# A mixture of experts over all experts, replaced by sorted pairs of token and expert with gathered rows

## The reference, cut to what matters

```python
def _L0_ffn_ref(x, Wr, br, W1, b1, W2, b2, ln_g, ln_b):     # D_MODEL = 768, D_HID = 192, N_EXP = 8
    logits = jnp.einsum('bsd,de->bse', x, Wr) + br
    probs = jax.nn.softmax(logits, axis=-1)
    top_vals, top_idx = jax.lax.top_k(probs, TOP_K)          # TOP_K = 2
    routing_weights = top_vals / jnp.sum(top_vals, axis=-1, keepdims=True)
    onehot = jax.nn.one_hot(top_idx, N_EXP, dtype=x.dtype)
    expert_weights = jnp.einsum('bsk,bske->bse', routing_weights, onehot)
    h = jax.nn.gelu(jnp.einsum('bsd,edh->besh', x, W1) + b1[None, :, None, :])
    y = jnp.einsum('besh,eho->beso', h, W2) + b2[None, :, None, :]
    out = jnp.einsum('beso,bse->bso', y, expert_weights)
    mu = jnp.mean(out, axis=-1, keepdims=True)
    var = jnp.mean(jnp.square(out - mu), axis=-1, keepdims=True)
    return (out - mu) * jax.lax.rsqrt(var + LN_EPS) * ln_g + ln_b
...
x = x + _L0_ffn_ref(_layernorm(x, axis=-1)[None], ...)[0]
```

## Time and profile before

| | us |
|---|---|
| median of 3 runs | 4639.31 (4627.12 to 4641.16) |
| profiled execution, its own time | 4635.16 |
| profiled execution, span from first to last instruction | 4633.4 |
| TensorE busy in the span | 3928.1 (85%) |
| VectorE busy | 2149.3 (46%) |
| GpSimd busy | 1350.2 (29%) |
| ScalarE busy | 1170.5 (25%) |
| mean granted clock of TensorE | 0.913 of 2.4 GHz |
| moved by DMA | 729.54 MB |

### The profile page before, as it was taken

One profiled execution on the slowest core, in us unless ns is written; L12 is line 12 of the kernel. 1 busy time (PEld: TensorE's weight loads), 2 busy tenths in 40 slices (PEclk: granted clock), 3 DMA queues, 4 the chain that ended last, 5 costly groups with the idle time before them and its releaser, 6 DMA issues. The chain is left out here.

```text
span 4633.4 us, 67390 instructions
## 1 busy us (share of the span) xinstructions
PE 3928.1 (85%) x23483; PEld 3147.0 (68%) x23484; DVE 2149.3 (46%) x4835; ACT 1170.5 (25%) x2391; POOL 1350.2 (29%) x1368
## 2 busy tenths in 40 slices
PE   6764988898989499996999578888878849999998
PEld 6763666666666288886999544554545449999997
DVE  6852555555555444443222144444444444444544
ACT  1231333333333233332111022222222122222222
POOL 1113655555556100000000144554555301111110
PEclk8886999999999799998999778888888969999999
DMA  5764666666676333334566466777777430000000
GB/s 207 255 247 140 222 208 216 212 216 216 215 223 215 118 139 135 140 124 127 80 80 77 151 226 220 257 250 238 259 229 241 148 117 21 27 20 20 27 20 13
DMA packets 239565, 729.54 MB, mean 157 GB/s; under 512 B 75503, under 2 KB 80650, under 8 KB 230995
## 3 DMA queue, kind: packets, MB, share of 16 engines
q0 software_dynamic: 88000, 374.95, 25.4%
q1 hardware_dynamic: 151315, 351.47, 25.0%
HBM read 642.07 MB, written 145.41 MB: 170 GB/s over the span
## 5 line engine op out<-in xcount | busy, mean ns | idle before, releaser
L873 POOL DMA_INDIRECT k_rows<-tab,k_pick x576 | 593.1, 1030 | 455.8 <-PE k_num L1293 307.7
L1996 POOL DMA_INDIRECT m_rows<-tab,m_e x500 | 486.6, 973 | 502.1 <-PE m_out L2295 313.7
L1293 PE MATMUL k_num<-k_rows,k_wt 128*64 128x385 f32 (+1 forms) x2400 | 435.8, 509 | 43.5 <-issue 38.6
L1293 PEld LDWEIGHTS k_num<-k_rows,k_wt 128*64 128x64 f32 x2400 | 171.8, 141 | 257.5 <-issue 239.7
L2275 PE MATMUL m_pj<-m_w,m_at 128*128 128x384 f32 x600 | 253.6, 582 | 28.8 <-DVE m_x L2091 22.7
L133 PE MATMUL g_prod<-g_w_hi,g_h_h 128*128 128x384 f32 x800 | 269.5, 337 | 1.5 <-DVE g_h_l L1594 1.5
L135 PE MATMUL g_prod<-g_w_hi,g_h_l 128*128 128x384 f32 x800 | 267.5, 334 | 0.0
L134 PE MATMUL g_prod<-g_w_lo,g_h_h 128*128 128x384 f32 x800 | 267.3, 334 | 0.0
L2295 PE MATMUL m_out<-m_rows,m_wt 128*32 128x384 f32 x2000 | 239.7, 513 | 22.7 <-issue 22.0
L133 PE MATMUL f_prod<-f_w_hi,f_a_h 128*128 128x512 f32 x600 | 243.9, 406 | 0.0
L2071 DVE TENSOR_REDUCE m_mx<-m_dash 128x2 f32<-128x512 f32 x150 | 103.0, 687 | 285.8 <-remote 205.5
(11 more groups left out here) (292 smaller groups left out, 8927.1 us busy)
## 6 DMA issues: line engine op xcount, KB each, us to landing
agg<-k_outb SPq DMA_DIRECT2D x100, 384.0 KB
f_a_in<-agg SPq DMA_DIRECT2D x100, 384.0 KB
h<-f_e SPq DMA_DIRECT2D x25, 1024.0 KB, 4.1
g_h<-h SPq DMA_DIRECT2D x25, 1024.0 KB, 12.9
tab<-q_xn SPq DMA_DIRECT2D x25, 388.5 KB, 6.0
tab<-g_row SPq DMA_DIRECT2D x25, 385.5 KB, 4.7
m_own<-tab SPq DMA_DIRECT2D x25, 385.5 KB
q_x<-in_x SPq DMA_DIRECT2D x25, 384.0 KB, 5.9
```

Of the source, the lines that this page charges most:

```text
L873: pool.indirect_dma_start(rows[:, place(u, n), :], None, dram["tab1"], at, bounds_check=bound, oob_is_err=False).then_inc(rows_in[i], 16)
L1293: mm = pe.matmul(num[i][64 * g:64 * g + 64, 0:n], wt[:, 2 * c + g, :], rows[:, place(u, 2 * c + g), a:a + n], start=(c == 0), stop=(c == 2 ...
L1996: pool.indirect_dma_start(rows[:, place(h, c) + k, :], None, tab, bass.IndirectOffsetOnAxis(ap=e[h % 4][:, 0, k * SLOTS + c:k * SLOTS + c ...
```

## The change

`phase_i` goes, and `phase_ffn` takes its place with three phases, each with a `Pool` and so a barrier of its own. All their loops are written out, with no loop instruction.

`phase_route` (tiles `r_`): for each of the 25 token tiles, layer norm, six transposes, copies to SBUF without splitting, and six float32 matmuls of 8 columns for the logits of the tile, which go to one PSUM bank for all tiles. The normalised rows are stored to HBM (`xn2`). Beside it the down weights are split in 16 pieces of 97 rows (96 rows of weights, and one of biases or its partner), and the up weights are loaded whole as float32 and not split. Then VectorE finds both experts and both weights of all tokens at once (tiles of 128 x 25 x 8), counts how many pairs come before each one (running sums over tiles, and TensorE products with a triangle and with ones for those over rows), rounds each expert's count up to whole tiles of 128, and so gives each pair a place. The list of tokens by place is made by 50 accumulated products of one-hot rows, half of which VectorE and half GpSimd makes. For each of the 56 tiles the expert's offset in the weights is stored (`up_at`, `down_at`).

`phase_experts` (tiles `e_`): 56 tiles of 128 places, whatever the counts. GpSimd gathers the rows of xn2 by the list into four buffers, TensorE transposes them, multiplies by the one expert's up weights in float32 (192 columns; the place in `w1` comes from a register that `value_load` fills), VectorE adds the bias and ScalarE applies gelu, two transposes of 96 columns turn the hidden rows, which are split, and 12 matmuls of 384 columns make the result, with the bias as a 97th row. The result is stored to HBM (`ys`).

`phase_combine` (tiles `o_`): for each token tile GpSimd gathers the two results of each token, ScalarE scales one, VectorE adds the other scaled, and the second layer norm and the sum follow as before.

The diff, cut to the loops of the three phases:

```diff
@@ phase_route
+            stats(0)
+            normed(0)
+            for t in range(NT):
+                if t + 1 < NT:
+                    stats(t + 1)
+                    normed(t + 1)
+                turned(t)
+                if t < len(JOBS):
+                    down_low(t)
...
+            dve.wait_ge(place_full, 1)
+            then(dve.scalar_tensor_tensor(out=at[:, :, :], in0=every(ends[:, 3:3 + NEXP]), scalar=float(P),
+                                          in1=place_b[:, 0:NT * NEXP].rearrange("p (t e) -> p t e", e=NEXP), op0=ALU.mult, op1=ALU.add))
...
+            for n in range(0, 2 * NT, 2):
+                if n >= 4:
+                    dve.wait_ge(listed, n - 3)
+                i, t = n // NT, n % NT
+                dve.tensor_scalar(spots[n % 4][:, :], iota[:, :], row[:, i, t:t + 1], ids[:, t:t + 1], ALU.is_equal,
+                                  ALU.mult).then_inc(even_done, 1)
...
+            for n in range(2 * NT):
...
+                pe.matmul(list_b[:, 0:ETILES], spots[n % 4][:, :], cols[:, n, :], start=(n == 0), stop=(n == 2 * NT - 1)).then_inc(listed, 1)
@@ phase_experts
+                pool.indirect_dma_start(x[j % R][:, :], None, dram["xn2"],
+                                        bass.IndirectOffsetOnAxis(ap=moe["list"][:, j:j + 1], axis=0)).then_inc(x_in[j % R], 16)
...
+            def up_product(j):
+                pe.wait_ge(first_done, j + 1)
+                pe.wait_ge(second_done, j + 1)
+                if j >= 2:
+                    pe.wait_ge(biased, j - 1)
+                at = pe.value_load(moe["up_at"][0:1, j:j + 1], min_val=0, max_val=(NEXP - 1) * DHID)
+                for k in range(KC):
+                    mm = pe.matmul(up[j % 2][:, 0:DHID], xt[j % 2][:, k, :], w1[:, k, bass.ds(at, DHID)], start=(k == 0), stop=(k == KC - 1))
+                mm.then_inc(up_full, 1)
...
+            turns(0)
+            for j in range(ETILES + 1):
+                if j < ETILES:
+                    up_product(j)
+                if j + 1 < ETILES:
+                    turns(j + 1)
+                if j >= 1:
+                    down_product(j - 1)
+                if j < ETILES:
+                    hidden_turns(j)
@@ phase_combine
+            for t in range(NT):
+                shifted(t)
+                layernorm_rstd(pool, mv, vps, rstd, keep["ln_eps"], keep["minus_half"], mean_done, vps_done, rstd_done, t)
+                if t + R - 1 < NT:
+                    gathers(t + R - 1)
@@ build
-        phase_i(nc, io, dram, keep, out)
+        phase_ffn(nc, io, dram, keep, out)
```

More of the change, by code:

```diff
@@ L43 @@
 DHID = 192
+HC = DHID // 2
+ETILES = (2 * N + NEXP * (P - 1)) // P
 CTXW = HEADS * 2 * VW
@@ L2325, in _ @@
                         heads_out(t, 5)
[L2329 to L2349, removed]
-        st, mv, vps, rstd = s.sb("st", [P, 2, 6]), s.sb("mv", [P, 2]), s.sb("vps", [P, 1]), s.sb("rstd", [P, 1])
[L2351 to L2357, removed]
-        up = [s.bank(f"up{i}") for i in range(2)]
-        down = [s.bank(f"down{i}") for i in range(2)]
-        c_in, x_in, out_sem = s.sem("c_in"), s.sem2("x_in"), s.sem2("out")
-        (stats_done, stats_seen, mean_done, vps_done, rstd_done, xn_done, turn_full, hi_done, lo_done, log_full, route_step, ew_steps,
-         exp_done, ew_done, ewt_full, ewt_done, up_full, biased, gelu_done, scaled, ht_full, hth_done, htl_done, down_full,
-         y_done, ystats_done, ystats_seen, ymean_done, yvps_done, yrstd_done, gain_done, sum_done, xs_done) = (
@@ L2415, in _ @@
-            tile_pairs(pool, step)
+            pool.wait_ge(row_done, 1)
+            pool.wait_ge(c_in, 16 * CONSTS)
+            for n in range(1, 2 * NT, 2):
+                if n >= 4:
+                    pool.wait_ge(listed, n - 3)
+                i, t = n // NT, n % NT
+                pool.tensor_scalar(spots[n % 4][:, :], iota[:, :], row[:, i, t:t + 1], ids[:, t:t + 1], ALU.is_equal,
+                                   ALU.mult).then_inc(odd_done, 1)
         @blk.scalar
         def _(act):
-            def high(t, b, g, first):
-                act.wait_ge(turn_full, t * 2 + g + 1)
-                if g == 0 and not first:
-                    act.wait_ge(up_full, t * 4 - 4)
-                act.activation(xt_h[b][:, 3 * g:3 * g + 3, :].rearrange("p k n -> p (k n)"), turn[g][:, 0:384],
-                               ACT.Copy).then_inc(hi_done, 1)
@@ L2462, in _ @@
+            act.wait_ge(gap_done, 1)
+            act.activation(second[:, :], second[:, :], ACT.Exp).then_inc(exp_done, 1)
         @blk.vector
         def _(dve):
[L2464 to L2476 removed]
@@ new lines, in _ @@
+            for k in range(5):
+                a, b = scan[k % 2], scan[(k + 1) % 2]
+                ins = dve.tensor_tensor(b[:, PAD:, :], a[:, PAD:, :], a[:, PAD - (1 << k):PAD + NT - (1 << k), :], ALU.add)
+                if k < 4:
+                    then(ins)
+            ins.then_inc(scan_done, 1)
+            then(dve.tensor_scalar(past[:, :], ids[:, :], float(N), None, ALU.is_ge))
+            dve.wait_ge(exp_done, 1)
+            then(dve.tensor_scalar(den[:, :], second[:, :], 1.0, None, ALU.add))
```

675 lines of the change are left out of this document (428 added, 247 removed).

## The result

The changed kernel takes 4364.1 us (median of 4 runs, 4348.2 to 4377.2) against 4639.2 for the kernel before, a ratio of 0.9412 (95% interval 0.9381 to 0.9443): 275 us less. The forecast was 4395, in a range of 4320 to 4520. The profiled execution of the changed kernel has a span of 4375.4 us, and its own first load of token tiles is issued at 3737.7 us, 18 us later than the corresponding load of before, although nothing ahead of it was changed. From there to the end it is 637.7 us, where the kernel before had 913.5. So the part that changed gives 275.8 us, as much as the medians differ by. One timed run of a later kernel, the one with stages loaded ahead, took 12733 us at a clock of 0.58 and is left out.

The account below looks back on a forecast made before the run. TensorE was taken to bound the replaced part of 913.5 us. Route 152, experts 355 and combine 163 sum to 670 us, a gain of 244, so 4639 - 244 = 4395 us, with an 80% range of 4320 to 4520.

Parts of the forecast that it names:

- Experts, the float32 products: Up products in experts: six float32 products of 192 columns at 0.17 us each, 1.0 us a tile.
- Experts, the register loads: Loads of the expert's place in experts: 0.5 us shows ahead of up, 0.3 ahead of down, each tile.
- Experts, transposes: TensorE's six transposes of x in each expert tile: 0.85 us.
- Experts, the clock: TensorE's clock in experts at 0.8 to 0.87, a third of the time low: 6.1 us a tile for 5.4.
- Experts as a whole: The experts stage: 56 tiles of 6.1 us, 342, plus 13 for its start and end, 355 us.
- Route: The route stage: 115 us to the last logits plus 37 for places, list and barrier, 152 us.
- so they hide. So does the DMA: In route's loop, TensorE's some 3 us a tile and the DMA's 88 us of 113 hide behind VectorE.
- Combine: The combine stage: GpSimd sets the pace at 5.85 us a tile, 163 us in all.
- a low clock throughout: Rival, 22%: in experts the clock stays low or all register work shows, 8.3 us a tile, kernel 4518 us.
- a bound by data movement: Rival, 8%: data movement at 216 GB/s bounds route (+24 us) and combine (+35 us), kernel 4454 us.
- tiles that do not overlap: Rival, 4%: phases of an expert tile do not overlap, 12.7 us a tile, kernel slower at 4765 us.
- The one with the sequencer hiding everything: Rival, 6%: register work hidden in experts, clock high, 4.5 us a tile, combine at the DMA's 4.6, kernel 4275 us.

Follow-up runs that it names:

- stages loaded ahead: The changed kernel with route's down-weight pieces loaded two tiles ahead, into five stages for three: 25 normalisations within 95.1 us, route 153.9 us for 166.9.
- fixed places: The changed kernel with each expert tile's place in the weights a constant in place of three register loads: 4.90 us a tile for 4.92.
- the tile was shortened: The changed kernel with one of six up products and each tile's place in the weights a constant, both at once: 3.52 us a tile for 4.92.
- the kernel with one up product: The changed kernel with only the first of a tile's six up products: 4.28 us a tile, 0.64 less.

## Why the prediction was right, and by which errors

The sum of 670 us was 32 too high, 5% of the part and 0.7% of the kernel. What bounds the kernel and what the change takes away were right. That the number came so near is luck: the terms were further off, route 15 us too low, experts 60 too high, combine 12 too low, and within the experts some 65 us too low and some 120 too high met.

- *What bounds the kernel, the 913.5 us, and that nothing ahead of them changes by the edit:* right. TensorE's work was the bound, the part fell from 913.5 to 637.7.
- *Experts, the float32 products:* wrong. The step that failed is "ten float32 products of 384 columns take 3.49 us, 0.33 apart". The ten are records, and a product is two of them: mix_out writes 300 such products and its line counts 600. The prediction itself had named 0.3 us for such a product with the clock high as a sign of being wrong, and it came. The six up products cost 1.95 us a tile and not 1.0; 56 tiles make it 53 us. The rule of the Trainium skill (FP8 and Floating Point Precision, TensorE Precision Notes) that I set aside, four passes for true FP32, is borne out: 0.325 us for 192 columns is 1.69 ns a column, four cycles of 2.4 GHz, against the 0.175 us for 384 columns of the split kind in the earlier trace rows. The estimate by that rule, +60 us, was good.
- *Experts, the register loads:* wrong by 0.8 us a tile, 45 us the other way, and the address operations by another 0.24, 13 us. What I priced as shown is hidden (fixed places: 0.02 us a tile), because the load ahead of up is over 0.7 us before TensorE gets to the hidden transposes that stand ahead of it. The price was real: 0.76 us of it came onto the path when the tile was shortened.
- *Experts, transposes:* 0.85 forecast, 0.58 measured, 15 us over 56 tiles. The row that I took, six in 1.01 us, is of the hidden rows; six of x in the kernel before take 0.82, as in the changed kernel (`4191.28 0.82 PE L2602 MATMUL i_turn<-keep_ident,i_xn 128*128 128x128 f32 x6`). Why the first took longer no run shows.
- *Experts, the clock:* wrong by 0.7 us a tile (6.1 for 5.4), 39 us. The clock was at 0.92 in the first 100 us, 1.00 in the next. Low it stood only at the start, as in the earlier trace rows: from 3921 to 4180 us it is 1.00.
- *Experts as a whole:* 355 forecast, 295 measured. With the clock high I had 5.4 us a tile: less 0.8 and 0.24 for the register work, plus 0.95, less 0.27 and 0.08 for the transposes (hidden ones 0.22 for 0.3), plus 0.09 for the down products (2.19 for 2.1) and less the 0.11 by which I had rounded up, it is 4.94. The start and end of the stage took 20 us for 13.
- *Route:* 152 forecast, 167 measured. The loop's 4.7 and 3.8 us a tile (106 us) came out at 108.6, but this is luck. VectorE's chain is shorter than forecast, 4.23 and 3.36 us a tile where nothing else holds it, and loads of weight pieces issued too late made up the difference. "so they hide. So does the DMA" was the step that failed: the DMA did not. VectorE was not the busy engine of the stage either: TensorE was busy 79 us of 100 and VectorE 63. The logits' end took 9.6 us for 2.5, again because a float32 product is two records and the clock is low. The 45 steps of VectorE on all tokens were right, 17.5 us for 18: 0.37 us for 200 elements, starts 0.40 apart. The list was 21.7 us for 16, within the bounds of 9 to 33.
- *Combine:* 163 forecast, 175.5 measured, 6.29 us a tile for 5.85. GpSimd sets the pace as forecast, and the queue order named (gathers and shift between two rstd) is the one found. In the terms of the sum, from the means between 4230 and 4350 us: the addition 1.81 us for 1.9, the two steps for rstd 1.49 (0.92 + 0.57) for 1.33, and the two gathers 2.93 with the gaps before them (2.44 + 0.49) for 2.5. So the largest error is the gathers, 1.22 us each where the earlier trace rows has 0.94; most of the rest is the hold-up by VectorE's scaling, of which the earlier trace rows had already put 1.14 us into the forecast. Why a gather takes longer here was not tried.
- *The rivals:* a low clock throughout, a bound by data movement and tiles that do not overlap did not come. The one with the sequencer hiding everything (6%, 4.5 us a tile) had the right mechanism for the register work and the right clock, and was too low by the float32 products; its combine at the transfers' 4.6 us a tile did not come in this kernel.

## What to carry to other kernels

Check a line's count against what the program writes before taking a duration per instruction from it: here a float32 product was two records, and half its price was missing. The register work of a tile cost 0.02 us while matmuls were queued ahead of it, and 0.76 us once it followed a wait that ended last. By that a register load belongs ahead of the wait, which no run here tried; this kernel has it behind, and gets away with it as long as other work separates the two. Work that nothing overlaps (the logits' end 9.6, places 17.5, list 21.7 us) was 29% of the route stage here: 49 us, as much as 10 expert tiles. A total that comes out right proves none of its terms; the experiments that take one term away do.

## What the runs showed of the hardware

- Experts and combine repeat within 1 us in all profiles in which they are not edited, on every chip; route within 3.4. mix_out does not. The first load of route came at 3719 to 3763 us in six profiles (the changed kernel's first one, and those on chips 1 and 9) and at 3587 to 3599 us in seven on chips 5 and 8. In the changed kernel the gathers of mix_out start within 882 us on chip 8 (2652.2 to 3534.4) and within 1050 in its first profile (2635.2 to 3685.5). The kernel before differs alike, 4639, 4656 and 4650 us against 4503 and 4506. What makes it so was not tried; the ratio of the changed kernel to it, 0.9412 and 0.9384, differs little.
- TensorE kept a clock of 1.00 with 10% idle time in two gaps of half a microsecond a tile, and with 15% in the kernel with one up product. In route, with transposes and products of 8 columns, its records have it busy 79% of the time, and 90% with the stages loaded ahead, and the clock stayed at 0.50.
- Beside GpSimd's elementwise addition of two tiles a step of VectorE on two tiles took 2.04 us for 1.02; the addition itself took 1.81 us, no more than the 1.91 of the earlier trace rows. A one-column step of GpSimd that met such a step of VectorE ended only with it (0.92 us for 0.19).
